# One operation for both halves of the clip and the first seeds, and an earlier place for the row's integers, in a GRU, attention, Runge-Kutta and quantised FFN kernel

## The reference

```python
def _derivative(q, p, drive, coupling, bias):
    i_couple = jnp.tanh(q) @ coupling.T
    dq = q - q ** 3 / 3.0 - p + drive + i_couple + bias
    dp = EPSILON * (q + ALPHA - BETA * p)
    return (dq, dp)

def _rk4_step(q, p, drive, coupling, bias):
    dq1, dp1 = _derivative(q, p, drive, coupling, bias)
    dq2, dp2 = _derivative(q + 0.5 * DT * dq1, p + 0.5 * DT * dp1, drive, coupling, bias)
    dq3, dp3 = _derivative(q + 0.5 * DT * dq2, p + 0.5 * DT * dp2, drive, coupling, bias)
    dq4, dp4 = _derivative(q + DT * dq3, p + DT * dp3, drive, coupling, bias)
    q_next = q + DT / 6.0 * (dq1 + 2 * dq2 + 2 * dq3 + dq4)
    p_next = p + DT / 6.0 * (dp1 + 2 * dp2 + 2 * dp3 + dp4)
    return (jnp.clip(q_next, -CLAMP, CLAMP), jnp.clip(p_next, -CLAMP, CLAMP))

def act_quant(x):
    scale = 127.0 / jnp.clip(jnp.max(jnp.abs(x), axis=-1, keepdims=True), EPS, None)
    return jnp.clip(jnp.round(x * scale), -128.0, 127.0) / scale

def bitlinear(x, w):
    return jnp.einsum('bsd,od->bso', act_quant(x), weight_quant(w))

gate = jax.nn.silu(bitlinear(x, w_gate))
up = bitlinear(x, w_up)
return bitlinear(gate * up, w_down)
```

## Time and profile before

| | |
|---|---|
| median of 3 runs | 619.08 us (618.81 to 619.54) |
| profiled execution | 620.08 us |
| its span | 618.2 us |
| PE busy | 582.3 us, 94% |
| PEld busy | 525.3 us, 85% |
| DVE busy | 518.4 us, 84% |
| ACT busy | 407.9 us, 66% |
| POOL busy | 255.7 us, 41% |
| share of the chain of waits | PE 63%, DVE 16%, ACT 14% |
| granted TensorE clock | 0.997 of full speed |
| length of a Runge-Kutta step | 9.17 us (L801 starts at 484.85, 494.02 and 503.19) |

### The profile page before, as it was taken

The page is one execution under the profiler, slowest core; times in us unless marked ns, Lnnn a source line. Parts: engine busy times, 40 slices in busy tenths (PEclk is TensorE's granted clock), DMA queues, the critical chain, the costliest instruction groups (busy, mean ns, idle before and its releaser), DMA issues.

```text
span 618.2 us, 14209 instructions
## 1 busy us (share of the span) xinstructions
PE 582.3 (94%) x4918; PEld 525.3 (85%) x4918; DVE 518.4 (84%) x1544; ACT 407.9 (66%) x968; POOL 255.7 (41%) x401
## 2 busy tenths in 40 slices
PE   8899999999999889988888999999999999999997
PEld 7899999999999878877776887887887888888875
DVE  3777777777777768888988999999999999999996
ACT  2544454545454465567447888888888889888885
POOL 0333333332322453420154455565565565565550
PEclk9999999999999999989999999999999999999999
DMA  8400000000000000500000000000000000000001
GB/s 270 165 2 2 1 1 2 1 1 2 1 1 1 19 1 1 185 1 1 2 0 2 10 14 15 19 19 10 19 19 10 20 18 10 19 19 10 19 19 34
DMA packets 12517, 14.87 MB, mean 24 GB/s; under 512 B 1632, under 2 KB 10144, under 8 KB 12448
## 3 DMA queue, kind: packets, MB, share of 16 engines
q1 hardware_dynamic: 12448, 13.97, 6.7%
HBM read 9.78 MB, written 4.19 MB: 23 GB/s over the span
## 4 chain that ended last, share of the span: by engine, by line
PE 63%; DVE 16%; ACT 14%; issue 4%; SPq 1%; DMA 1%; POOL 0%; ACTq 0%; DVEq 0%
PE PS L451 18%; PE PS L313 16%; PE PS L336 12%; ACT q_s L761 4%; PE PS L505 3%; PE PS L527 3%; ACT k_s L740 2%; PE PS L489 2%; PE PS L372 2%; PE PS L429 2%; ACT big L672 2%; PE PS L389 2%; ACT q_s L801 2%; DVE h_s L1059 1%; DVE big L941 1%
## 5 line engine op out<-in xcount | busy, mean ns | idle before, releaser
L451 PE MATMUL PS<-k_s,h_s 128*128 128x128 f32 x1024 | 163.4, 287 | 4.7 <-DVE PS L1039 2.1
L451 PEld LDWEIGHTS PS<-k_s,h_s 128*128 128x128 f32 x1024 | 131.6, 191 | 24.7 <-DVE PS L1047 9.5
L313 PE MATMUL PS<-part 128*128 128x256 f32 x900 | 115.6, 286 | 0.6 <-issue 0.6
L313 PEld LDWEIGHTS PS<-part 128*128 128x128 f32 x900 | 109.8, 191 | 0.8 <-issue 0.8
L740 ACT ACTIVATE k_s<-h_s 128x128 f32<-128x128 f32 x256 | 71.3, 305 | 32.6 <-DVE h_s L1059 25.3
L336 PE MATMUL PS<-big,wrk 128*128 128x128 f32 x744 | 88.4, 275 | 3.0 <-DVE big L898 3.0
L336 PEld LDWEIGHTS PS<-big,wrk 128*128 128x128 f32 x744 | 85.8, 192 | 3.6 <-DVE big L898 3.6
L1207 POOL COPY h_s<-big 128x256 f32<-128x256 f32 x32 | 21.5, 671 | 130.8 <-DVE big L898 130.8
L451 PE MATMUL PS<-h_s 128*128 128x128 f32 x384 | 74.2, 275 | 0.0
L451 PEld LDWEIGHTS PS<-h_s 128*128 128x128 f32 x384 | 58.3, 192 | 0.0
L637 ACT ACTIVATE big<-big 128x256 f32<-128x256 f32 x32 | 13.3, 417 | 65.5 <-DVE big L880 65.5
(11 more groups left out here) (184 smaller groups left out, 1269.1 us busy)
## 6 DMA issues: line engine op xcount, KB each, us to landing
out<-q_s SPq DMA_DIRECT2D x32, 128.0 KB, 1.7
x_s<-in_xT SPq DMA_DIRECT2D x14, 256.0 KB, 5.9
k_s<-in_wgT SPq DMA_DIRECT2D x1, 832.0 KB, 6.1
k_s<-in_wuT SPq DMA_DIRECT2D x1, 832.0 KB, 7.8
k_s<-in_wih SPq DMA_DIRECT2D x3, 256.0 KB, 4.0
wrk<-in_whh SPq DMA_DIRECT2D x3, 256.0 KB, 4.4
h_s<-in_wdT SPq DMA_DIRECT2D x1, 768.0 KB, 7.8
x_s<-in_xT SPq DMA_DIRECT2D x4, 128.0 KB, 3.6
```

The lines of the kernel that those rows point to most:

```text
L313: r = pe.matmul(p, y, x, start=i == 0, stop=i == len(passes) - 1)
L451: return pe.matmul(PS[:, m, 0:128], w, x, start=False, stop=True, skip_group_check=True)
```

## The change

Three things change, all in the Runge-Kutta loop.

1. The clip at the end of a step is one operation over both banks, which waits for both updates (`s_next` at `8 * t + 8`) and raises `s_q` by 2.
2. The seeds of slot 0 are one operation over both banks, which raises `s_seed` by 2.
3. The rounding of the row's integers on ScalarE moves from behind slot 2's tanh to ahead of them, right behind the copy L767. The two transposes on TensorE move from the middle of slot 2 to ahead of it, right behind the products L505. The reciprocal moves from between slot 2's seeds to behind the second seed of slot 1, ahead of slot 1's cubic.

```diff
-            def coupled(slot, scale=None, x=None, between=None):
+            def coupled(slot, scale=None, x=None):
...
-                    if between is not None and m == 0:
-                        between()
...
-                def turn_integers():
+                if t:
                     pe.wait_ge(s_qf, t)
                     for k in range(2):
                         r = pe.transpose(cm(pqi, k), low(cm(qf, k)), identh[:, :])
                     r.then_inc(s_turnqi, 1)
-
-                coupled(4 * t + 2, id_s2, qs[0], turn_integers if t else None)
+                coupled(4 * t + 2, id_s2, qs[0])
...
-            def stage(slot, between=None):
+            def stage(slot):
...
-                if between is not None:
-                    between()
...
-                stage(4 * t + 2, (lambda: integers(t - 1)) if t else None)
+                if t:
+                    integers(t - 1)
+                stage(4 * t + 2)
...
-                for m in range(2):
-                    if t:
-                        ve.wait_ge(s_next, 8 * t - 1 + m)
-                    ve.tensor_tensor(PS[:, m, 0:128], I_at(t)[:, m], cm(pn[t % 2], m), ALU.subtract).then_inc(s_seed, 1)
+                if t:
+                    ve.wait_ge(s_next, 8 * t)
+                ve.tensor_tensor(PS[:, 0:2, 0:128], I_at(t), two(pn[t % 2]), ALU.subtract).then_inc(s_seed, 2)
...
                 seed_2(t, 1)
+                if t >= 1:
+                    ve.wait_ge(s_tq, t)
+                    ve.reciprocal(q_at(t - 1, 4), q_at(t - 1, 1)).then_inc(s_s1, 1)
...
                 seed_3(t, 0)
-                if t >= 1:
-                    ve.wait_ge(s_tq, t)
-                    ve.reciprocal(q_at(t - 1, 4), q_at(t - 1, 1)).then_inc(s_s1, 1)
                 seed_3(t, 1)
...
-                for m in range(2):
-                    ve.wait_ge(s_next, 8 * t + 7 + m)
-                    ve.tensor_scalar(cm(qn[(t + 1) % 2], m), PS[:, m, 128:256], CLAMP, -CLAMP, ALU.min,
-                                     ALU.max).then_inc(s_q, 1)
+                ve.wait_ge(s_next, 8 * t + 8)
+                ve.tensor_scalar(two(qn[(t + 1) % 2]), PS[:, 0:2, 128:256], CLAMP, -CLAMP, ALU.min, ALU.max).then_inc(s_q, 2)
```

## The result

The changed kernel takes 621.46 us in the median of 11 runs (621.12 to 622.50), the kernel before 619.08 us (618.60 to 621.66). The ratio is 1.0037 (95% interval 1.0028 to 1.0046): the change makes the kernel 0.37% slower. The forecast was 618.5 us and no measurable difference. The profiled execution of the changed kernel took 621.32 us, with a span of 619.5 us.

The account below looks back on a forecast made before the run. Each 9.17 us step was taken as bound by ScalarE at its start, then TensorE. 0.11 - 0.04 - 0.09 = -0.02 a step, times 28, is -0.6 us: median 618.5 us from 619.08, range 616.4 to 621.2.

Parts of the forecast that it names:

- the start of the clip: Step boundary on VectorE: second half's update ends at 503.19, plus a hand-over of 0.03, so the merged clip starts at 503.23.
- the tanh's shift: ScalarE's first tanh of a step moves from 503.57 to 503.68, +0.11 us; square, L761 and L489 follow it unchanged.
- Rival 2: The clip's wait dominates: clip starts no earlier than 503.30, tanh at 503.76, +0.06 a step, 620.8 us; chance 0.18.
- s: Shift of the step's first tanh against before, in us; forecast 0.11, faster needs under 0.09, slower over 0.175.
- far end: Rival 2's extreme: clip takes 676 ns like L855, s = 0.37, +0.24 a step, 625.8 us.
- s - 0.13 a step: Change of one step's length, linear in the tanh's shift s; the 0.13 is 0.04 from slot 1 and 0.09 from slot 2.
- The integers' move: TensorE's slot 2: with the integers' transposes ahead of it, 1.50 instead of 1.59, -0.09 us a step.
- Rounding and reciprocal: Rounding ends by 507.66, free on ScalarE; reciprocal costs VectorE 0.07 ahead of slot 1's cubic, covered by waits for TensorE.
- Slot 1 absorbs 0.04: About 0.04 of TensorE's slot 1 was waiting for a tanh, so it shifts by 0.07 instead of 0.11.
- The seeds cost nothing: Merged seeds in slot 0 on VectorE end about 503.98, as does the tanh that the same first product needs.
- the rule on few chained operations: Trainium skill's advice to minimise chained VectorE operations; by that alone the four-to-two merge gives 0.13 times 31, -4.0 us.
- Rival 1: Larger operations pay: 256-column clip takes 281 ns, s = 0, -0.13 a step, 615.4 us; chance 0.07.

Follow-up runs that it names:

- e1: Changed kernel with merged clip and merged seeds raising their semaphores by 1 instead of 2, waits counted accordingly; 619.91 us, ratio 0.9996 to the kernel before.
- e6: Kernel before with only the updates raising their semaphore s_next by 2 instead of 1, waits counted accordingly; 626.36 us, ratio 1.0120.
- e2: Kernel before with only the move of integers, their transposes and the reciprocal; clip and seeds stay in halves; 616.49 us, ratio 0.9955 to the kernel before.
- e3: Kernel before with only the merged clip and merged seeds, raising by 2; integers in their old place; 624.28 us, ratio 1.0082 to the kernel before.
- e4: Changed kernel with the clip again in two halves; seeds stay merged, integers stay moved; 617.24 us, ratio 0.9957 to the kernel before.
- e8: e4 with the wait for the up products named first at VectorE's product L1066; 616.25 us, ratio 0.9957 to the kernel before.
- e9: e8 with the waits also reordered at the transposes L487 (rounding first) and the rescaling (transposes of x first); 614.08 us, ratio 0.9911 to the kernel before.
- e7: e9 with the products of slots 0 and 1 also naming the tanh's wait before the seed's; 617.13 us, ratio 0.9966 to the kernel before.
- e5: Changed kernel with slot 3's update written to an SBUF tile that the clip reads; clip raises by 1, seeds by 2; 618.61 us, ratio 0.9982 to the kernel before.
- e10: e2 run again, the same kernel, beside e9 on one chip; 618.21 us, ratio 0.9974 to the kernel before.
- e11: e8 run again, the same kernel, beside e9 on one chip; 614.70 us, ratio 0.9925 to the kernel before.

## Why the prediction was wrong

**The step that failed** is the start of the clip: "503.19, plus VectorE's own hand-over. That one is 0.03 ... So it starts at 503.23." The hand-over of 0.03 was read from an operation that carries its own wait. The merged clip raises `s_q` by 2 and so its wait is an instruction by itself, which the chain shows between update and clip, 0.02 and an issue of 0.05. That puts the clip 0.41 behind the update instead of 0.34. With a raise by one the forecast's 0.34 comes out (e1); with a raise by two in a kernel that is otherwise the one before, the same 0.07 appears at the updates (e6).

**The rest of the tanh's shift.** I had +0.11; measured it is 0.19 (0.87 against 0.68). The separate wait is 0.07 of the 0.08 between them. The remaining 0.01 lies in the clip's length, 0.424 at the upper end of my 0.41 to 0.42. One more term was missing: the second tanh starts 0.217 behind the first now and 0.200 before. ScalarE came straight from L801 before, and now sits idle ahead of the first tanh. So the square and L756 come 0.207 later, not 0.11.

**Rival 2 came nearest**: it had the clip at 503.30, s = 0.19 and 620.8 us. That its s came out is luck. I argued it as "no row shows an earlier start"; the cause is the raise, which I had not looked at. Its far end doesn't follow from its own start either: 503.30, 0.68 and 0.03 give s = 0.44, and the 0.37 is counted from 503.23. The formula behind the sum, s - 0.13 a step, held: with s = 0.207 it gives +0.077, and the step grew by 0.07. Times 28 that is 2.0 us, against the 2.4 of the medians. Of the 2.4, the loop shows 1.8 (302.7 against 300.9) and the stretch behind the last tanh 0.2 (619.5 - 603.4 against 618.2 - 602.3); the other 0.4 is not in the two traces. The two profiled executions are only 1.3 apart, since the loop of the one before begins 0.7 later (301.4 against 300.7).

**Right in the forecast:**

- The integers' move, -0.09 a step: e2 has it alone, and e3 against the changed kernel has it from the other side. Slot 2 is undivided, 0.11 and 1.39, and followed by L524.
- Rounding and reciprocal are covered: slot 2's tanh is released by slot 1's update, not by the rounding, and TensorE doesn't wait for it.
- Slot 1 absorbs 0.04: its first weight load stands at the last transpose (506.46), as forecast, and the slot takes 1.39 instead of 1.43.
- The seeds cost nothing. They gain nothing either, and that I had for the wrong reason in part. I weighed the rule on few chained operations only against the idle time in front of the clip. In e4, where this idle time is gone, it still gives nothing, because the separate wait for the up products holds the product L1066. With that wait named first (e8), the step falls by 0.04.
- Rival 1 fell: the clip takes 0.42, not 0.28.

**Wrong in the range.** Its upper end, 621.2, lies 0.26 below the measured 621.46. The bound on the hand-over was missing: I had one value (0.03) for it, and only the clip's length had two ends.

**With a raise of one** the result is e1's, 9.17 and 0.9996. The forecast of -0.02 a step is then off by 0.02, the two small terms above.

**Open.** Why the separate wait costs 0.07 on VectorE and how ScalarE's 0.217 arises is in no row. Whether the chip or the tool that builds the program takes the wait out of an operation that raises by two isn't shown, and raises by other numbers were not tried. The three reordered waits were not run singly, except the product's. A version of e9 with the merged clip was not run.

## What to carry to other kernels

Raise a semaphore by one in every operation on the path, and let those who wait count in that unit: a raise by two put a separate wait of 0.07 us ahead of the operation. Where an operation waits for several things, name first the one that is fulfilled last, and find out from the trace which one it is at each place, since e7 lost part of its gain by one wrong guess. Before merging two operations over halves, ask what the second half's wait does to the first: here even the merged clip with a raise by one lets the tanh go only 0.80 behind the update (e1), 0.12 later than the two halves did.

## What the runs showed of the hardware that I had not expected

- A wait that its operation doesn't carry costs 0.07 us on VectorE (e1 against the changed kernel; e6) and 0.06 on TensorE's weight load (e7's 0.11 against e9's 0.05). An operation that raises by two doesn't carry its wait even if it has only one (the changed kernel, e6).
- The clip of 128x256 takes 0.42 from PSUM and 0.29 from SBUF, but 0.37 from SBUF while GpSimd works beside it for the first 0.22 (e5).
- ScalarE's second tanh of a step follows the first by 0.217 if ScalarE was idle before it (after, e1, e3), by 0.200 if not (before, e9).
- In some executions TensorE's granted clock drops in the first half: 0.66 as the mean between 266 and 270 in e10, that is 0.34 x 4 / 0.5 = 2.7 us at 1.2 instead of 2.4 GHz. TensorE is little busy there, 2.56 of 4.00 us in e10 and 2.34 in e11, where the same first half keeps its clock at 1.00. Executions of the kernel before with a mean clock of 0.997 took 1.7 us longer in the median than those with 1.000 (620.32 against 618.65). A comparison within 0.3% should go by the length of the changed loop.
